# Graph network kernel: block joins in five parts, and SAGE's own linear part moved into the adjacency products

## The chip, the cores and the metric

The kernel runs on one core of a Trainium2 chip. The metric is the device time of one execution in microseconds (us), the median of several runs.

## The reference

The program is a stack of six graph layers over N = 3125 nodes with 128 features and E = 50000 edges, which are sorted by destination:

```
x  = x + relu(batchnorm(A x W0 + b))                 # GCN
x  = x + ffn(norm(attn(x, edge_attr)))               # 8 heads x 16, softmax over a node's edges
x  = x + gat1/gat2(x)                                # 3 heads x 128, then 1 head x 128
for l in (sage1, sage2):
    agg = segment_sum(h[src], dst) / max(cnt, 1)
    y   = agg @ Wl.T + h @ Wr.T + b
    h   = (y - mean) * (gamma / sqrt(var + eps)) + beta   # relu between the two
x  = x + h
```

attn, gat1 and gat2 have this form for each edge: a logit from the source's and the destination's rows, then, for every destination, sum(exp(logit - max) * row) / sum(exp(logit - max)).

## The kernel before, in words

The nodes are 25 tiles of 128; node stages go over them in seven turns (`TURNS`: one tile, then six times four). The edges are 392 blocks of 128 (`CH`), four blocks are a group (`GC`, 98 groups), two groups a pair (`NPR` = 49 ticks).

**An edge pass** (attn, gat1, gat2) is a software pipeline written out by hand. Each engine has a list of steps with an offset, for example `(terms, 2, 0)`, and `ticks` runs the whole list once for each pair: a step with 2 handles one group of the pair, one with 1 the pair. The steps of one pair in program order on DVE are `maxima` (the running maximum of a destination's logits, two scans, L2257 and L2263), `terms` of the even group (attn: L2224 adds the edge terms from PSUM to the gathered k and v rows, L2227 multiplies by the query rows from PSUM, L2243 reduces; gat: L2234 adds and L2247 applies the leaky slope), `difs` (L2270), `terms` of the odd group, and `messages` of the two groups of the pair before (L2286). PE makes the edge terms (`edge_terms`, L1573, attn only), spreads destination rows over edges (`dst_rows`, L1584 in attn, L1589 in gat), transposes the maxima (`max_t`, L1604) and sums the messages of a block (`sums`, L1613). ACT moves those sums out of PSUM (a copy, L1052), takes exponents (L1189), and stores them to memory (L1167). SP loads the constants of each group (L804, L811, L816, L819).

POOL gathers the source rows of a group from memory, four indirect loads (L1021). There are eight buffers of rows; the gather of group n waits for the messages of group n-8.

A destination's edges may run over several blocks. Each block leaves the sum and the maximum of its first and its last destination, and after the last group one **join** over all 392 blocks puts them together: PE collects the edge maxima (L1626), DVE makes the running maximum over the blocks and its differences (L2300 to L2316, `span` steps), ACT takes the exponent (L1221), SP loads the first and last rows of each block that were stored (L631), PE spreads the weights over partitions (L1642) and transposes the rows (L1659), and DVE runs for the denominators and for each chunk of 128 columns (attn and gat2 one chunk, gat1 three) two products, a scan, a product and a sum (L2328 to L2335). PE turns the result back (L1668, L1671), ACT copies it and SP stores it. Only then does POOL gather the result row of each node (L1030), and the node stage begins.

```
ticks([(maxima, 1, -1), (terms, 2, 0), (difs, 1, -1), (terms, 2, 1), (messages, 2, -2), (messages, 2, -1)])
```

**PSUM** has eight banks. In attn, bank 1 and bank 6 hold the edge terms of even and odd groups; in gat, banks 3 and 1 hold the destination rows of even and odd groups. A step that writes a bank waits for DVE's step of the group two before.

**SAGE** multiplies by the adjacency matrix in ten column chunks (`stream`, L1540; nine of them 100 matmuls long, in pieces of 5 tiles). After the product, a node stage goes over the turns: PE transposes h (L1690), multiplies the aggregate by Wl and the transposed h by Wr (L1809), ACT divides by the count (`mean_in`, L1355), DVE adds the two, multiplies by the batch norm's factor and adds its offset (L2537, L2381 twice). In sage1 the result is then split into three bfloat16 parts for the next product; in sage2 it is added to x and stored.

## Time and profile before

| | us |
|---|---|
| median of 3 runs | 3554.34 (3553.38 to 3568.37) |
| profiled execution, its own time | 3551.71 |
| its span | 3550.1 |

| stage | from | to |
|---|---|---|
| attn pass, its join | 660 | 1412, 1443.9 |
| gat1 pass, its join | 1571 | 2268.8, 2312.1 |
| gat2 pass, its join | 2445 | 3097, 3128.6 |
| gat2's node stage and the first SAGE product | 3128.6 | 3320 |
| sage1's node stage | 3338.0 | 3357.4 |
| second SAGE product | 3357.4 | 3507.7 |
| sage2's node stage, end | 3525.5 | 3550.1 |

Busy: PE 69%, DVE 40%, POOL 38%, ACT 27% of the span; the mean granted clock is 0.743 of full speed. The stage times are read off the timeline. A row of the timeline gives the start, the duration, engine, line and shape, and in brackets how long the engine stood idle before it and what released it ("remote" is a releaser that the trace doesn't identify).

### The profile page before, as it was taken

The numbers are of one execution on the slowest core, as the hardware profiler recorded it, in microseconds if no ns is written. First come the engines' busy times: TensorE is split into PE (matmuls) and PEld (weight loads), VectorE is DVE, ScalarE is ACT, GpSimd is POOL, SyncE is SP. The second block draws the span as 40 slices with busy tenths as digits, with TensorE's granted clock in tenths as the row PEclk, the third lists the DMA queues.
The fourth block names the chain that finished last, engine by engine and source line by source line (L and its number), as shares of the span: only waits on it lengthen the run. The fifth ranks groups of instructions, "written<-read, shape, count | busy, mean of one in ns | idle before, by whom it ended". The sixth has DMA issues, their size and how long they took to land.

```text
span 3550.1 us, 36582 instructions
## 1 busy us (share of the span) xinstructions
PE 2464.1 (69%) x12427; PEld 1828.4 (52%) x12427; DVE 1418.4 (40%) x3070; ACT 962.5 (27%) x2050; POOL 1354.0 (38%) x1417
## 2 busy tenths in 40 slices
PE   4999997377666766545677666664565655649998
PEld 3666665256555555333444444443564555526666
DVE  6756555244444455533333333431221212251423
ACT  3422223122222222442333333231221222220202
POOL 3000002645444553375555555045565555320000
PEclk9777788677777787667888888776555555569999
DMA  9388641456666674124555655322344444346362
GB/s 210 115 300 297 234 147 39 139 167 189 175 177 180 177 199 142 26 55 125 169 184 172 189 181 186 107 70 52 88 112 95 106 105 103 94 137 205 116 205 66
DMA packets 518595, 517.78 MB, mean 146 GB/s; under 512 B 154128, under 2 KB 463763, under 8 KB 517227
## 3 DMA queue, kind: packets, MB, share of 16 engines
q1 hardware_dynamic: 310349, 267.24, 24.9%
q0 software_dynamic: 50528, 115.22, 13.3%
q10 hardware_dynamic: 157534, 132.98, 11.9%
q8 instruction: 102, 1.67, 0.2%
q14 instruction: 82, 0.67, 0.1%
HBM read 301.13 MB, written 227.33 MB: 149 GB/s over the span
## 4 chain that ended last, share of the span: by engine, by line
PE 40%; another core or an unknown queue 25%; DVE 12%; issue 12%; ACT 6%; DMA 2%; POOL 1%; ACTq 0%; DVEq 0%; SPq 0%
PE ps L1613 9%; PE ps L1540 8%; PE ps L1434 6%; PE ps L1444 5%; ACT arena L1052 4%; DVE arena L2224 2%; DMA ends_gat<-arena 1%; PE ps L1522 1%; DVE arena L2286 1%; PE ps L1589 1%; PE ps L1573 1%; PE ps L1584 1%; DVE arena L1934 1%; DVE arena L2227 1%
## 5 line engine op out<-in xcount | busy, mean ns | idle before, releaser
L1052 ACT ACTIVATE arena<-ps 128x544 f32<-128x544 f32 (+9 forms) x591 | 485.9, 825 | 1746.1 <-remote 874.5
L1613 PE MATMUL ps<-arena 128*128 128x136 f32 (+2 forms) x2352 | 695.9, 460 | 376.3 <-ACT arena L1052 194.6
L1021 POOL DMA_INDIRECT arena<-t_gat,src_i x784 | 741.9, 946 | 537.1 <-DVE arena L2286 307.8
L1613 PEld LDWEIGHTS ps<-arena 128*128 128x128 f32 x2352 | 479.6, 269 | 516.4 <-issue 425.2
L1021 POOL DMA_INDIRECT arena<-t_attn,src_i x392 | 375.4, 958 | 344.1 <-DVE arena L2286 225.3
L2257 DVE TENSOR_TENSOR_SCAN arena<-arena,ps 64x128 f32<-64x128 f32 (+2 forms) x147 | 60.0, 408 | 803.0 <-remote 714.2
L1540 PE MATMUL ps<-arena 128*128 128x384 bf16 x1850 | 308.2, 331 | 37.6 <-issue 25.1
L1589 PEld LDWEIGHTS ps<-arena 128*128 128x128 f32 x1568 | 288.3, 268 | 45.2 <-issue 22.5
L1589 PE MATMUL ps<-arena 128*128 128x3 f32 (+1 forms) x1568 | 266.6, 292 | 15.7 <-issue 15.7
L1540 PEld LDWEIGHTS ps<-arena 128*128 128x128 bf16 x1850 | 183.1, 99 | 162.4 <-issue 46.0
L2286 DVE TENSOR_TENSOR arena<-arena,ps 128x1536 f32<-128x1536 f32 (+1 forms) x196 | 230.6, 1218 | 38.7 <-ACT arena L1189 30.1
L1444 PE MATMUL ps<-arena 128*128 128x100 bf16 x1176 | 224.4, 364 | 9.4 <-DVE arena L2064 9.2
L1434 PE MATMUL ps<-arena 128*128 128x385 bf16 x925 | 221.0, 413 | 0.0
L984 POOL TENSOR_TENSOR arena<-arena,r_L_gnn_gamma 128x512 f32<-128x512 f32 (+1 forms) x7 | 8.1, 1158 | 533.4 <-ACT arena L1252 533.3
L1444 PEld LDWEIGHTS ps<-arena 128*128 128x128 bf16 x1176 | 169.3, 145 | 58.9 <-DVE arena L2064 12.6
L1573 PE MATMUL ps<-w_e,arena 64*128 64x128 f32 x784 | 148.6, 324 | 59.7 <-issue 59.2
L1604 PE MATMUL ps<-ident,arena 64*128 64x64 f32 (+2 forms) x147 | 40.8, 278 | 201.1 <-DVE arena L2263 164.9
L2270 DVE TENSOR_TENSOR dif<-logit,ps 128x64 f32<-128x64 f32 (+2 forms) x147 | 27.4, 187 | 374.9 <-remote 199.5
L1052 ACT ACTIVATE arena<-same_b 128x512 f32<-128x512 bf16 x294 | 167.7, 619 | 29.6 <-DMA same_b<-same_hbm 28.7
L1573 PEld LDWEIGHTS ps<-w_e,arena 64*128 64x128 f32 x784 | 120.4, 222 | 88.5 <-issue 88.4
L1434 PEld LDWEIGHTS ps<-arena 128*128 128x128 bf16 x925 | 112.2, 121 | 102.9 <-issue 68.9
L1052 ACT ACTIVATE arena<-arena 128x512 bf16<-128x512 f32 (+4 forms) x208 | 64.3, 309 | 346.1 <-DVE arena L2524 247.8
(320 smaller groups left out, 2942.1 us busy)
## 6 DMA issues: line engine op xcount, KB each, us to landing
ends_gat<-arena ACTq DMA_DIRECT2D x98, 774.0 KB
arena<-adj_hbm SPq DMA_DIRECT2D x90, 640.0 KB, 4.2
same_b<-same_hbm SPq DMA_DIRECT2D x294, 128.0 KB
adj_hbm<-arena SPq DMA_DIRECT2D x9, 3200.0 KB, 11.8
ends_attn<-arena ACTq DMA_DIRECT2D x98, 272.0 KB
ends_gat<-arena ACTq DMA_DIRECT2D x98, 258.0 KB
arena<-edst SPq DMA_DIRECT2D x98, 256.0 KB, 4.2
starts_q<-zrow SPq DMA_DIRECT2D x28, 896.0 KB, 6.8
```

The lines of the kernel that those rows point to most:

```text
L1021: g.indirect_dma_start(out=row_b[:, n % RB, k, 0:row_tab[p].shape[1]], out_offset=None, in_=row_tab[p], in_offset=bass.IndirectOffsetOnAxi ...
L1052: return a.activation(o, i, ACT.Copy)
L1434: i = mm(bank(4 + n % 4)[:, 0:3 * D + 1], lhs, xs0[:, t, 0:3 * D + 1], start=t == 0, stop=t == NT - 1)
L1444: i = mm(ps[:, at:at + KEYS], hot_e[:, b % 3, :, e], hot_k[:, b % 3, :, e], start=True, stop=True)
L1540: m = mm(bank(ch % 2 * 4 + dl)[:, 0:3 * D], ring[:, u % RING, at:at + P], xs1[:, t, :, :].rearrange("p s c -> p (s c)"), start=t == 0, sto ...
L1573: i = mm(bank((1, 6)[g % 2])[:, k * D:(k + 1) * D], at_t[:, g % 2, k * P:(k + 1) * P], w_e[:, :], start=True, stop=True)
L1589: i = mm(ps[:, at:at + n_er], same_f[:, g % RB, k, :], er_c[:, g * GC + k, 0:n_er], start=True, stop=True)
L1604: nc.tensor.transpose(bank(2)[:, 256:256 + kh], mx[0:kh, i % 2, :], ident[0:kh, 0:kh])\
L1613: i = mm(o, same_f[:, g % RB, k, :], msg[:, g % 4, k * W:(k + 1) * W], start=True, stop=True)
L2224: tt(kv, kv, bc(bank((1, 6)[g % 2]).rearrange("p (k s c) -> p k s c", k=GC, s=1), [P, GC, 2, D]), ALU.add).then_inc(kve_done.sem, 1)
L2257: v.tensor_tensor_scan(fwd[0:kh, s, :], b[:, 0:P], bank(2)[0:kh, 0:P][:, ::-1], -BIG, ALU.add, ALU.max)\
L2286: tt(m[:, :, 0:heads * nc_].rearrange("p k (h c) -> p k h c", h=heads), rows_v, e, ALU.mult).then_inc(msg_done.sem, 1)
```

## The change

1. **Joins in five parts.** The blocks are cut at 72, 144, 216, 288 and 392. Four parts are joined inside the pass, at groups that `slots_of` lists; a step `mini` in each engine's list of the tick runs what is due there. A part is `edges` and the first transposes (PE), `tops` (DVE), the exponent (ACT), `mask` and the first `join` (DVE), then for each chunk transposes and spread (PE), a copy (ACT) and a `join` (DVE), then `back` (PE) and the rows' copy (ACT) and store (SP). A `carry` column hands the running values on. The fifth part, 104 blocks, is joined after the pass. SP loads the part's first and last rows in the pass and stores the results there.
2. **PSUM.** The parts inside the pass need a bank. In attn the edge terms now have only bank 1 and wait for L2224 of the group before; in gat1 the destination rows have only bank 3 and wait for L2234 of the group before. gat2 keeps both. In PE's list `max_t` moves ahead of these steps.
3. **SAGE.** The transposes of h and the product with Wr move ahead of the pieces of the first chunk (`own_lin`, called from `stream`). A new DVE step `keep` puts that product plus the batch norm's offset into h_sb, and the second chunk waits for the last `keep`. The batch norm's factor is multiplied into both weights once. What is left of the node stage is the product with Wl and one DVE instruction for each tile, which multiplies by the count's inverse and adds (`joined_in`); ACT's `mean_in` is gone, and in sage2 the product with Wl has two banks.

```diff
+PARTS = [(0, 72), (72, 144), (144, 216), (216, 288), (288, CH)]
+QP = len(PARTS)
+PW = max(b - a for a, b in PARTS)
...
+        def slots_of(p):
+
+            slots = {}
+
+            def put(g, *step):
+                slots.setdefault(g, []).append(step)
+
+            for q in range(QP - 1):
+                s = PARTS[q][1] // GC + 7
+                put(s, "edges", q, 0)
+                put(s + 1, "tops", q, 0)
+                put(s + 2, "exp", q, 0)
+                put(s + 3, "mask", q, 0)
+                put(s + 3, "join", q, 0)
+                for ch in range(1, col_chunks(p) + 1):
+                    put(s + 1 + 3 * ch, "cols", q, ch)
+                    put(s + 2 + 3 * ch, "copy", q, ch)
+                    put(s + 3 + 3 * ch, "join", q, ch)
+                s += 4 + 3 * col_chunks(p)
+                put(s, "back", q, 0)
+                put(s + 1, "rows", q, 0)
+            assert max(slots) < NG
+            return slots
...
+                def rows_for(q):
+                    b0, b1 = PARTS[q]
+                    g1 = b1 // GC
+                    for g in (g1 - 2, g1 - 1):
+                        sp.wait_ge(ends_out.of(g), ends_out.at(p, g))
+                    if part_at(p, q) > 1:
+                        sp.wait_ge(col_ps, col_at(p, q, 0) - 1)
+                    sp.dma_start(z_rows[0:b1 - b0, 0:W], v_ends[b0:b1, 0, :]).then_inc(s_rows, 16)
+                    sp.dma_start(f_rows[0:b1 - b0, 0:W], v_ends[b0:b1, P - 1, :]).then_inc(s_rows, 16)
+
+                def sums_out(q):
+                    b0, b1 = PARTS[q]
+                    sp.wait_ge(col_out, back_at(p, q, col_chunks(p)))
+                    sp.dma_start(ends[p][EP + P + b0:EP + P + b1, :], r_rows[0:b1 - b0, 0:W]).then_inc(s_rout, 16)
+
+                rows_at = {PARTS[q][1] // GC + 10: q for q in range(QP - 1)}
+                out_at = {PARTS[q][1] // GC + 19 + 3 * col_chunks(p): q for q in range(QP - 1)}
                 for g in range(NG):
                     if g % 2 == 0:
                         load_breaks(g // 2)
                     load_group(g)
-                for g in (NG - 2, NG - 1):
-                    sp.wait_ge(ends_out.of(g), ends_out.at(p, g))
-                sp.wait_ge(s_steps, c.at("z_in"))
...
                 def edge_terms(g):
                     pe.wait_ge(attr_sb_done.sem, attr_sb_done.at(p, g))
-                    if g >= 2:
-                        pe.wait_ge(kve_done.sem, kve_done.at(p, g, 2))
+                    if g >= 1:
+                        pe.wait_ge(kve_done.sem, kve_done.at(p, g, 1))
                     for k in range(GC):
-                        i = mm(bank((1, 6)[g % 2])[:, k * D:(k + 1) * D], at_t[:, g % 2, k * P:(k + 1) * P], w_e[:, :],
+                        i = mm(bank(1)[:, k * D:(k + 1) * D], at_t[:, g % 2, k * P:(k + 1) * P], w_e[:, :],
                                start=True, stop=True)
                     i.then_inc(e_done.sem, 1)
 
                 def dst_rows(g):
                     pe.wait_ge(same_f_done.sem, same_f_done.at(p, g))
-                    if g >= 2:
-                        pe.wait_ge(prod_done.sem, prod_done.at(p, g, 2))
+                    back = 1 if p == "gat1" else 2
+                    if g >= back:
...
-                    ticks([(logit_t, 1, -1), (sums, 2, -4), (attr_t, 2, 2), (edge_terms, 2, 1), (dst_rows, 2, 1),
-                           (max_t, 1, -1), (sums, 2, -3), (attr_t, 2, 3), (edge_terms, 2, 2), (dst_rows, 2, 2)])
+                    ticks([(logit_t, 1, -1), (sums, 2, -4), (attr_t, 2, 2), (max_t, 1, -1), (edge_terms, 2, 1),
+                           (dst_rows, 2, 1), (sums, 2, -3), (attr_t, 2, 3), (mini, 2, 0), (edge_terms, 2, 2),
+                           (dst_rows, 2, 2), (mini, 2, 1)])
...
+                    ticks([(logit_t, 1, -1), (sums, 2, -4), (max_t, 1, -1), (dst_rows, 2, 1), (sums, 2, -3),
+                           (mini, 2, 0), (dst_rows, 2, 2), (mini, 2, 1)])
...
-                ticks([(maxima, 1, -1), (terms, 2, 0), (difs, 1, -1), (terms, 2, 1), (messages, 2, -2), (messages, 2, -1)])
...
+                def tops(q, ch=0):
+                    b0, b1 = PARTS[q]
+                    n, k0, o = b1 - b0, span_at(p, q), Psum(p, q)
+
+                    def after(m):
+                        dve.wait_ge(span_dve, k0 + m)
+
+                    cpen, lpen = (span_m[0:heads, 2 + s, :] for s in range(2))
+                    R, M = run_x[0:heads, :], top_m[0:heads, 0:n]
+                    ex = lambda e: ex_h[0:heads, e, 1:n + 1]
+                    dve.wait_ge(edge_m_ps, part_at(p, q))
+                    after(0)
+                    if q == 0:
+                        v.memset(R[:, 0:1], -BIG)
+                        v.memset(ex_h[0:heads, :, 0:1], 0.0)
+                        v.memset(carry[:, :], 0.0).then_inc(span_dve, 1)
+                        after(1)
+                        v.tensor_tensor_scan(R[:, 1:n + 1], cpen[:, 0:n], o.last[:, 1:n + 1], -BIG, ALU.add, ALU.max)\
+                            .then_inc(span_dve, 1)
+                    else:
+                        m = PARTS[q - 1][1] - PARTS[q - 1][0]
+                        v.tensor_copy(o.last[:, 0:1], R[:, m:m + 1]).then_inc(span_dve, 1)
+                        after(1)
+                        v.tensor_tensor_scan(R[:, 0:n + 1], cpen[:, b0 - 1:b1], o.last, -BIG, ALU.add, ALU.max)\
+                            .then_inc(span_dve, 1)
+                    after(2)
+                    tt(ex(0), R[:, 0:n], R[:, 1:n + 1], ALU.subtract)
+                    tt(ex(1), o.last[:, 1:n + 1], R[:, 1:n + 1], ALU.subtract)
+                    tt(M, R[:, 0:n], lpen[:, b0:b1], ALU.add).then_inc(span_dve, 1)
+                    after(3)
+                    tt(M, M, o.first, ALU.max).then_inc(span_dve, 1)
+                    after(4)
...
+                def mask(q, ch=0):
+                    b0, b1 = PARTS[q]
+                    e = ex_h[0:heads, ::3, 1:b1 - b0 + 1]
+                    dve.wait_ge(span_exp, part_at(p, q))
+                    tt(e, e, span_m[0:heads, 0:2, b0:b1], ALU.mult).then_inc(span_dve, 1)
...
+                    dve.wait_ge(col_ps, col_at(p, q, ch))
+                    dve.wait_ge(span_dve, k0)
+                    if col_at(p, q, ch) > 1:
+                        dve.wait_ge(col_done, col_at(p, q, ch) - 1)
+                    if ch == 0 and part_at(p, q) > 1:
+                        dve.wait_ge(col_back, back_at(p, q, 0) - 1)
+                    if ch >= 2 and q == QP - 1:
+                        dve.wait_ge(col_back, back_at(p, q, ch - 2))
+                    held = carry[0:parts_n, ch:ch + 1]
+                    v.tensor_copy(u[:, 0:1], held)
+                    tt(u[:, 1:n + 1], e[:, 1, 1:n + 1], z, ALU.mult)
+                    tt(t, e[:, 2, 1:n + 1], f, ALU.mult).then_inc(span_dve, 1)
+                    dve.wait_ge(span_dve, k0 + 1)
+                    v.tensor_tensor_scan(sc[:, 0:n + 1], e[:, 0, 0:n + 1], u[:, 0:n + 1], 0.0, ALU.mult, ALU.add)\
+                        .then_inc(span_dve, 1)
+                    dve.wait_ge(span_dve, k0 + 2)
+                    tt(u[:, 1:n + 1], e[:, 3, 1:n + 1], sc[:, 0:n], ALU.mult)
+                    v.tensor_copy(held, sc[:, n:n + 1]).then_inc(span_dve, 1)
+                    dve.wait_ge(span_dve, k0 + 3)
+                    tt(t, t, u[:, 1:n + 1], ALU.add).then_inc(col_done, 1)
+
+                def mini(g):
+                    in_slots(p, g, tops=tops, mask=mask, join=join)
+
+                ticks([(maxima, 1, -1), (terms, 2, 0), (difs, 1, -1), (terms, 2, 1), (mini, 2, 0), (messages, 2, -2),
+                       (messages, 2, -1), (mini, 2, 1)])
+                tops(QP - 1)
...
+                own, at_piece = own_lin(i), [0, 2, 6, 8, 10, 12, 14]
                 for n, (ch, t0, t1) in enumerate(PIECE):
+                    if n <= NT // HI:
+                        for step, j in own[at_piece[n]:at_piece[n + 1]]:
+                            step(j)
+                    if (ch, t0) == (1, 0):
+                        pe.wait_ge(dve_o.sem, dve_o.at(("gat2", "sage1")[i], "keep"))
...
+                def la(j):
+                    if p == "sage1" and j >= 1:
+                        pe.wait_ge(dve_o.sem, dve_o.at(p, "yh", j - 1))
+                    if p == "sage2" and j >= 2:
+                        pe.wait_ge(dve_o.sem, dve_o.at(p, "yx", j - 2))
+                    b = 7 if p == "sage1" else 6 + j % 2
+                    for k, t in enumerate(range(*TURNS[j])):
+                        m = mm(part(bank(b), k), part(agg_t, t), sage_t[:, 2 * i, :], start=True, stop=True)
+                    m.then_inc(pe_o.sem, 1)
+
...
+            for i in range(2):
+                k = tt(sage_t[:, 2 * i:2 * i + 2, :], sage_t[:, 2 * i:2 * i + 2, :],
+                       bc(bn_a[:, i:i + 1, :], [P, 2, D]), ALU.mult)
+            k.then_inc(s_sage, 1)
+
+            def own_sum(i, stage, after):
+                def step(j):
+                    dve.wait_ge(pe_o.sem, pe_o.at(stage, "lh", j))
+                    dve.wait_ge(dve_o.sem, dve_o.at(after, "r2", j))
+                    tt(tiles(h_sb, j), in_bank(6)(j), fb(bn_b[:, i, :], j), ALU.add).then_inc(dve_o.sem, 1)
+                return step
 
...
+                def joined_in(b, t_out):
+                    def step(j):
+                        dve.wait_ge(pe_o.sem, pe_o.at(p, "la", j))
+                        if p == "sage2":
+                            dve.wait_ge(s_sage, 2)
+                        for k, t in enumerate(range(*TURNS[j])):
+                            n = stt(t_out[:, t, :], part(bank(b(j)), k), cnt_r[:, t:t + 1], t_out[:, t, :], ALU.mult, ALU.add)
+                        n.then_inc(dve_o.sem, 1)
+                    return step
+
```

PE, one tick of attn before and after (in the rows L1613 is `sums`, L1565 `attr_t`, L1573 `edge_terms`, L1584 `dst_rows`, L1604 `max_t`, L1597 `logit_t`; after, these are L1751, L1702, L1710, L1722, L1742, L1735). Before:

```order
L1597 MATMUL ps<-ident,logit 64x128
L1613 MATMUL ps<-arena 128x136 x4
L1565 MATMUL ps<-ident,arena 64x128 x4
L1573 MATMUL ps<-w_e,arena 128x128 x4
L1584 MATMUL ps<-arena 128x128 x4
L1604 MATMUL ps<-ident,arena 128x64
L1613 MATMUL ps<-arena 128x136 x4
L1565 MATMUL ps<-ident,arena 64x128 x4
L1573 MATMUL ps<-w_e,arena 128x128 x4
L1584 MATMUL ps<-arena 128x128 x4
```

After, in a tick with the end of a part (L1809 and L1810 are `back`):

```order
L1735 MATMUL ps<-ident,logit 64x128
L1751 MATMUL ps<-arena 128x136 x4
L1702 MATMUL ps<-ident,arena 64x128 x4
L1742 MATMUL ps<-ident,arena 128x64
L1710 MATMUL ps<-w_e,arena 128x128 x4
L1722 MATMUL ps<-arena 128x128 x4
L1751 MATMUL ps<-arena 128x136 x4
L1702 MATMUL ps<-ident,arena 64x128 x4
L1809 MATMUL ps<-ident,ht 72x128
L1810 MATMUL ps<-ident,ht 72x8
L1710 MATMUL ps<-w_e,arena 128x128 x4
L1722 MATMUL ps<-arena 128x128 x4
```

The first `edge_terms` and `dst_rows` of a tick stood ahead of `max_t` and now stand behind it; `back` stands between the second `sums` and the second `edge_terms`.

DVE, the end of one tick of attn, where L2286 is `messages`. Before:

```order
L2270 TENSOR_TENSOR dif<-logit,ps 128x64
L2224 TENSOR_TENSOR arena<-arena,ps 128x1024
L2227 TENSOR_TENSOR arena<-arena,ps 128x512
L2243 TENSOR_REDUCE logit<-arena 128x32
L2286 TENSOR_TENSOR arena<-arena 128x4x128 x2
L2257 SCALAR_TENSOR_TENSOR arena<-arena,ps 64x128
```

After, in the tick with part 0's `tops` (L2460 to L2483); `messages` is L2445 there:

```order
L2460 MEMSET arena 8x1
L2461 MEMSET arena 8x4
L2462 MEMSET arena 128x4
L2464 SCALAR_TENSOR_TENSOR arena<-span_m,ps 8x72
L2473 TENSOR_TENSOR arena<-arena 8x72
L2474 TENSOR_TENSOR arena<-ps,arena 8x72
L2475 TENSOR_TENSOR arena<-arena,span_m 8x72
L2477 TENSOR_TENSOR arena<-arena,ps 8x72
L2479 TENSOR_TENSOR arena<-ps,arena 8x72
L2480 TENSOR_TENSOR arena<-arena 8x72
L2483 TENSOR_SCALAR arena<-arena 8x4x72
L2445 TENSOR_TENSOR arena<-arena 128x4x128 x2
```

The eleven rows of `tops` come ahead of the messages of the tick.

PE around the node stage of sage1 before (L1690 transposes h, L1809 multiplies), and the product behind it:

```order
L1809 MATMUL ps<-sage_t,arena 128x128 x4
L1809 MATMUL ps<-sage_t,ht 128x128 x4
L1690 MATMUL ps<-ident,h_sb 128x128 x4
L1809 MATMUL ps<-sage_t,arena 128x128 x4
L1809 MATMUL ps<-sage_t,ht 128x128 x4
L1540 MATMUL ps<-arena 128x384 x925
```

PE at the first chunk of the first product after (L1644 transposes h, L1654 multiplies by Wr, L1677 is the product):

```order
L1644 MATMUL ps<-ident,h_sb 128x128 x5
L1677 MATMUL ps<-arena 128x384 x20
L1654 MATMUL ps<-sage_t,ht 128x128
L1644 MATMUL ps<-ident,h_sb 128x128 x4
L1654 MATMUL ps<-sage_t,ht 128x128 x4
L1644 MATMUL ps<-ident,h_sb 128x128 x4
L1677 MATMUL ps<-arena 128x384 x20
L1654 MATMUL ps<-sage_t,ht 128x128 x4
```

The product of 20 matmuls (five tiles) of the first chunk now stands between a turn's own product and the next.

## Rows read from the trace of the kernel before

**Rows 1.** The page: the clock by slices, and POOL's gather groups of part 5
```profile
PEclk9777788677777787667888888776555555569999
...
L1021 POOL DMA_INDIRECT arena<-t_gat,src_i x784 | 741.9, 946 | 537.1 <-DVE arena L2286 307.8
...
L1021 POOL DMA_INDIRECT arena<-t_attn,src_i x392 | 375.4, 958 | 344.1 <-DVE arena L2286 225.3
```

**Rows 2.** Busy time by stretch: the three joins (stretch, length, engines, clock, DMA)
```profile
core 0: us, PE busy (x) PEld busy (x) DVE busy (x) ACT busy (x) POOL busy (x), PEclk, DMA share, GB/s
1414.00:1444.00 30.00, 13.57 (x69) 9.02 (x68) 12.39 (x22) 5.69 (x6) 0.10 (x1) 0.50 0.14 40
2268.80:2312.10 43.30, 27.13 (x105) 16.39 (x104) 18.68 (x32) 9.16 (x9) 0.07 (x1) 0.57 0.24 79
3099.00:3128.60 29.60, 13.17 (x67) 8.60 (x66) 16.07 (x36) 5.65 (x6) 0.09 (x1) 0.50 0.14 39
```

**Rows 3.** Timeline in attn (start, us, engine, line, tiles, [idle before <-releaser])
```profile
1013.71 2.07 PE L1584 MATMUL ps<-arena 128*128 128x128 f32 x8 [0.34 <-issue]
...
1040.45 0.95 POOL L1021 DMA_INDIRECT arena<-t_attn,src_i  x1 [0.30 <-issue]
...
1042.82 0.37 PE L1573 MATMUL ps<-w_e,arena 64*128 64x128 f32 x1 [1.03 <-issue]
...
1044.25 1.62 PE L1584 MATMUL ps<-arena 128*128 128x128 f32 x6 [0.15 <-issue]
...
1044.36 0.41 DVE L2257 TENSOR_TENSOR_SCAN arena<-arena,ps 64x128 f32<-64x128 f32 x1 [14.45 <-remote]
...
1045.15 1.19 DVE L2224 TENSOR_TENSOR arena<-arena,ps 128x1024 f32<-128x1024 f32 x1
...
1045.80 0.37 PE L1604 MATMUL ps<-ident,arena 64*128 64x64 f32 x1
...
1046.10 2.18 PE L1613 MATMUL ps<-arena 128*128 128x136 f32 x8
...
1047.98 1.22 DVE L2224 TENSOR_TENSOR arena<-arena,ps 128x1024 f32<-128x1024 f32 x1
...
1049.06 1.16 PE L1573 MATMUL ps<-w_e,arena 64*128 64x128 f32 x8
...
1049.23 0.69 DVE L2227 TENSOR_TENSOR arena<-arena,ps 128x512 f32<-128x512 f32 x1
...
1051.99 0.94 POOL L1021 DMA_INDIRECT arena<-t_attn,src_i  x1 [10.59 <-DVE arena L2286]
```

**Rows 4.** Timeline in gat1, one critical tick
```profile
1834.09 0.99 PE L1589 MATMUL ps<-arena 128*128 128x3 f32 x8
...
1837.31 0.24 PE L1604 MATMUL ps<-ident,arena 24*128 24x24 f32 x1 [2.23 <-DVE arena L2263]
...
1837.70 0.17 DVE L2234 TENSOR_TENSOR z_b<-arena,ps 128x12 f32<-128x12 f32 x1
...
1840.90 0.95 POOL L1021 DMA_INDIRECT arena<-t_gat,src_i  x1 [7.20 <-DVE arena L2286]
```

**Rows 5.** Timeline in gat2, POOL's first gather after a wait
```profile
2700.90 0.95 POOL L1021 DMA_INDIRECT arena<-t_gat,src_i  x1 [6.40 <-DVE arena L2286]
```

**Rows 6.** Timeline of attn's join
```profile
1414.94 2.78 PE L1626 MATMUL ps<-arena,ident 64*8 64x49 f32 x32
...
1419.23 0.14 DVE L2303 TENSOR_TENSOR arena<-arena 8x1 f32<-8x1 f32 x1
...
1425.74 5.56 PE L1642 MATMUL ps<-arena,spread 8*128 8x392 f32 x8 [8.02 <-issue]
...
1431.23 2.77 PE L1659 MATMUL ps<-ident,arena 98*8 98x98 f32 x16
...
1438.11 0.57 DVE L2333 TENSOR_TENSOR arena<-arena 128x391 f32<-128x391 f32 x1
...
1443.90 0.95 POOL L1030 DMA_INDIRECT arena<-ends_attn,end_i  x1 [63.74 <-SPq L836]
```

**Rows 7.** Timeline of gat1's join, its first and last step and SP's load
```profile
2268.93 1.60 PE L1626 MATMUL ps<-arena,ident 24*3 24x49 f32 x32
...
2275.11 0.83 SPq L631 DMA_DIRECT2D arena<-ends_gat  x2
...
2312.03 0.95 POOL L1030 DMA_INDIRECT arena<-ends_gat,end_i  x1 [88.93 <-SPq L836]
```

**Rows 8.** Timeline of the SAGE node stages
```profile
3353.68 0.60 PE L1690 MATMUL ps<-ident,h_sb 128*128 128x128 f32 x4
...
3356.24 1.13 ACT L1355 ACTIVATE h_sb<-ps,cnt_r 128x128 f32<-128x128 f32 x4
...
3356.40 1.16 PE L1809 MATMUL ps<-sage_t,ht 128*128 128x128 f32 x8 [1.23 <-ACT ht L1052]
...
3357.39 2.93 PE L1540 MATMUL ps<-arena 128*128 128x384 bf16 x17
...
3545.29 0.69 DVE L2381 TENSOR_TENSOR x_sb<-h_sb,x_sb 128x512 f32<-128x512 f32 x1
```

462 lines of the change are left out of this document (258 added, 204 removed).

## Prediction

> **What bounds the kernel now.** I began with the page: no engine is busy over 69% of the span, so waits set the time in most stages. The costliest group of waits is POOL's ahead of its gathers, which DVE's messages end: 307.8 us in the two gat passes and 225.3 us in attn [rows 1]. The timeline of one tick of attn shows what such a wait is. POOL issues 16 gathers of four groups back to back, 0.95 us each and 0.30 us apart, 20 us in all; the last one starts at 1040.45. Meanwhile DVE stands still for 14.45 us, until 1044.36, 3 us after POOL's last gather has been issued; ACT and SP start again within 0.1 us of it. Then comes a tick that nothing covers, which I call the critical tick. DVE goes through its maxima (1044.36), the terms of the even group (1045.15) and of the odd group (1047.98 and 1049.23) with no gap over 0.1 us. POOL goes on after the first message, having waited 10.59 us [rows 3]. The next tick runs under the new burst. So a period of two ticks is a burst plus that wait, 30.6 us: what is added ahead of the messages of a critical tick lengthens the pass, and what is added elsewhere fits into DVE's 14 us. In gat1 the wait is 7.20 us [rows 4], in gat2 6.40 us [rows 5]. By the sums of rows 1, attn has about 225.3 / 10.59 = 21 such periods; gat1, which also has shorter waits, I put at 20, gat2 at 20.
>
> The joins are the second bound: 30.0, 43.3 and 29.6 us in which POOL, whose gathers the next stage needs, is idle [rows 2]. They are a chain of small steps through PE, DVE, ACT and SP, with PE at half clock (0.50 to 0.57).
>
> **The joins, after.** What is left after the pass handles 104 of 392 blocks. In attn the join runs from 1414.94 to POOL's gather at 1443.90. A DVE step takes 0.57 us for 391 elements and 0.14 us for one, so 1.1 ns for each element more; 104 elements take 0.25 us. The spread of the weights (5.56 us) shrinks to 1.6 us, the transposes of the rows (2.77 us for 16) to 0.7 us for 4 [rows 6]. The first step (2.78 us for 32 records) has as many matmuls as before, and the store and its landing (2.8 us, from ACT's copy to the gather) stay. My sum for what is left is 2.8 + 3.4 for the maxima + 1.6 + 0.7 + 0.6 for ACT's copy + 3.2 for DVE's two runs + 0.4 for turning back + 2.8 = 15.5 us, so 13.5 us saved. gat2 has the same form: 13.5 us. gat1 goes from 2268.93 to 2312.03; its rows are loaded from 2275.11 on [rows 7], and with four runs on DVE I come to 23 us, 20 saved. Together **-47 us**. If all but the first step and the store scaled with the blocks, it were -61; if only DVE and the spread did, -35.
>
> **The parts inside the passes.** By the same line a step of 72 elements takes 0.22 us, so `tops` is about 2.1 us on DVE, `mask` 0.25, and a `join` 1.45. Their slots fall now in a critical tick, ahead of the messages, now in a covered one. Counting slots against the ticks of the trace, three `tops` and two `mask` with `join` are exposed in attn (7 us less what falls behind messages), 11 us in gat1, which has three chunks, and 8 us in gat2: **+26 us**. The ends are 0 (every such tick turns into a covered one) and 75, the whole DVE work of 12 parts. I take 26, since rows 3 show DVE with no gap in a critical tick, and a long gap behind it. PE's and ACT's parts of this, and SP's two loads and one store for each part, I cost at nothing: PE, ACT and SP all stand still in the bursts as DVE does. If their cover is gone, see the last rival. Behind PE's wait for SP's load stand `edge_terms` and `dst_rows` of the next tick, and DVE's terms wait for those.
>
> **One bank and the new order on PE.** This I take to be the largest cost. Before, PE did the edge terms and destination rows of the odd group inside the stall: the edge terms end at 1043.19 and the destination rows at 1045.87, when DVE has just started [rows 3]. Now the edge terms of the odd group wait for DVE's L2224 of the even group, which ends at 1046.34, and stand behind `max_t`. PE has then been idle for the whole stall and is at half clock: eight records take 2.07 us there, against 1.16 us at full clock [rows 3]. So edge terms end at 1048.5 and destination rows at 1050.6 (half clock) or 1049.7 (full). DVE's L2224 of the odd group moves from 1047.98 to 1048.6, its L2227 from 1049.23 to between 1049.9 and 1050.7. The messages come 0.7 to 1.5 us later; I take 1.4, because in the rows PE stays at half clock through the sums that follow (2.18 us at 1046.10). That is 21 x 1.4 = 29 us, and 4 us in the ticks at the end of the pass, where POOL has no more gathers: +33. In gat1 the destination rows of the odd group took 0.99 us at 1834.09, in the stall. Now they follow `max_t`, which ends at 1837.55, and end at 1838.7; DVE's L2234 of that group started at 1837.70 [rows 4]. That is 1.1 us a period, 20 periods: +22. gat2 keeps two banks: 0. Together **+55 us**, between 0 and 75.
>
> **SAGE.** The work on PE is moved, not removed: 0.60 us of transposes and 1.16 us of products with Wr for four tiles, 11 us for a whole pass [rows 8]. What it lands in, the first chunk of the first product, is slack only where PE waits for the tiles to be ready, about 3 us. It then delays the second chunk by about 7 us in each product, since the second chunk also waits for the last `keep`. In sage1 those 11 us and ACT's 1.13 us a turn leave the node stage, where the first product's piece starts at 3357.39; I have the second chunk 1 us later than now at best and 7 later at worst, and take 7. sage2's node stage (3525.5 to the last sum at 3545.29) loses the transposes, ACT's step and three of four DVE steps of 0.69 us; 8.6 us stay, -12. Sum 7 + 7 - 12 = **+3 us** (from -10 to +10).
>
> **Sum**: -47 + 26 + 55 + 3 = +37. The profiled execution took 3551.7 us, 2.6 below the median of the runs; on the median this gives 3554.3 + 37 = 3591 us. About 0.5%, 18 us, is what a measurement of this kernel can tell from no change.
>
> **Rivals.**
> *All of it is covered (faster, 3510).* The work in the passes and PE's later steps cost nothing and only the joins get shorter: -47 + 3 = -44. It decides if the odd group's operands are in PSUM when DVE comes to them, that is if PE's two steps together take under 2.6 us (1046.34 to 1048.98), and if the parts' slots fall in covered ticks. For it: DVE is only 40% busy. Against it: the half clock in every stall [rows 3], and the slots. Chance 0.25.
> *PE runs at full clock after the stall (same, 3558).* Edge terms then end at 1047.6 and destination rows at 1048.8, both before DVE wants them, and attn's 33 us go; gat1's 22 stay: +4. Chance 0.2.
> *Descriptors are held up (3601).* In the trace a gather issued in a burst takes 958 ns in attn, where DVE works more, and 946 ns in gat [rows 1], so DVE's work holds POOL up by little. If the copies and scalar steps of the parts stopped POOL for their length, that would be about 0.9 us for a part in attn and gat2 and 1.4 in gat1, 13 us less the exposed third, +10 on the sum. The Trainium skill ("SBUF — State Buffer", section "Who interferes with whom") states such a lock: a DVE instruction in a two-port mode, as copies and tensor_scalar can be, shuts GpSimd out for its whole length. Rows 1 agree only in that tensor_tensor work costs next to nothing; what a copy does, none of them shows. Chance 0.05.
> *The loaded rows come late (slower, 3680).* PE waits in a tick for rows that SP loads while the gathers fill the queues, and these are released only when a burst is over, as DVE is in rows 3. With 12 parts and up to a critical tick (7.4 us) for each, +90. It decides if SP's load of a part is issued less than a burst ahead of PE's step. Chance 0.1.
>
> **Chances.** The forecast gets 0.4. Faster: the first rival's 0.25 and 0.05 from a forecast in which gat1 and the parts cost less: 0.3. Same: the second rival's 0.2, and 0.05 of the forecast. Slower: 0.45. The range of 3508 to 3630 goes from the first rival to the forecast with PE's term at its upper end (+75); it leaves out most of the last rival and of the still larger savings.
>
> **What would show it.** Right: joins of about 15, 23 and 15 us; POOL's wait in attn 12.0 us instead of 10.6 and in gat1 8.3; gaps of 0.6 us ahead of L2224's and L2227's successors in the critical tick with PE as releaser; edge terms of the odd group behind `max_t` at 2.07 us; sage2's node stage 12 us shorter; the first chunk of each product longer. Wrong: POOL's waits unchanged, or PE's steps at 1.16 us there (then the second rival), or waits on SP's loads in the passes.

## The result, and the profile after

The changed kernel takes **3622.12 us** (median of 4 runs, 3620.23 to 3626.14) against 3556.52 us before on the same chip: the ratio is 1.0188 (95% interval 1.0156 to 1.0219), 66 us slower. The profiled execution has a span of 3619.0 us, 68.9 more than before.

I cut both traces at the same events of the timeline: POOL's first gather of a pass, DVE's last message of it, POOL's first gather of the results, and PE's first matmul of the second chunk and last one of each product.

| stretch, us | before | after | difference |
|---|---|---|---|
| attn pass, first gather to last message | 747.5 | 805.1 | +57.6 |
| gat1 pass | 689.2 | 733.9 | +44.7 |
| gat2 pass | 647.5 | 661.9 | +14.4 |
| last message to first gather of the results, attn | 35.4 | 19.1 | -16.3 |
| the same, gat1 | 51.1 | 30.3 | -20.8 |
| the same, gat2 | 35.8 | 19.8 | -16.0 |
| gat2's results to the second chunk | 57.6 | 68.9 | +11.3 |
| end of the first product to the second chunk of the second | 53.6 | 63.0 | +9.4 |
| end of the second product to the end | 42.5 | 30.4 | -12.1 |
| everything else | 1189.9 | 1186.6 | -3.3 |

The passes lose 116.7 us, the joins win 53.1, SAGE loses 8.6.

The page after shows the clock of the slices and the gather groups, which answer to [rows 1]:

```profile
PEclk9777788677777777676878877877555555569999
...
L1111 POOL DMA_INDIRECT arena<-t_gat,src_i x784 | 741.6, 946 | 592.4 <-DVE arena L2445 363.5
...
L1111 POOL DMA_INDIRECT arena<-t_attn,src_i x392 | 373.2, 952 | 404.2 <-DVE arena L2445 285.3
```

POOL waits 285.3 us for messages in attn, 60 more than before, and 363.5 in the gat passes, 56 more. The gathers themselves take as long as before (946 and 952 ns).

The joins by stretch (the columns are those of [rows 2]), from the last message on:

```profile
1468.30:1487.20 18.90, 9.00 (x64) 7.16 (x62) 5.41 (x24) 4.68 (x8) 0.00 (x0) 0.50 0.24 68
2347.90:2378.20 30.30, 15.46 (x84) 10.73 (x84) 8.40 (x39) 6.50 (x11) 0.01 (x1) 0.70 0.35 121
3169.10:3188.90 19.80, 9.12 (x65) 7.27 (x64) 8.11 (x35) 4.61 (x8) 0.00 (x0) 0.50 0.22 62
```

Inside attn's join, from the timeline (start, us, engine, line):

```profile
1474.42 0.96 PE L1763 MATMUL ps<-arena,ident 64*8 64x13 f32 x32
...
1475.42 0.15 DVE L2468 COPY ps<-arena 8x1 f32<-8x1 f32 x1 [7.31 <-PE ps L1763]
...
1476.00 0.26 DVE L2473 TENSOR_TENSOR arena<-arena 8x104 f32<-8x104 f32 x1
...
1478.78 2.03 PE L1779 MATMUL ps<-arena,spread 8*128 8x105 f32 x8 [3.40 <-DVE arena L2489]
...
1480.75 0.85 PE L1798 MATMUL ps<-ident,arena 104*8 104x104 f32 x4
...
1487.25 0.94 POOL L1120 DMA_INDIRECT arena<-ends_attn,end_i  x1 [47.08 <-DMA ends_attn<-arena]
```

From PE's first step to POOL's gather it is 12.8 us, where it was 28.96 [rows 6]. A DVE step of 104 elements takes 0.26 us, the spread 2.03 and the transposes 0.85 us. PE's first step writes 13 columns instead of 49, so its 32 records take 0.96 us, not 2.78.

A tick of attn that nothing covers, again from the timeline, which answers to [rows 3]:

```profile
1227.53 0.94 POOL L1111 DMA_INDIRECT arena<-t_attn,src_i  x1 [0.30 <-issue]
...
1230.80 0.41 DVE L2416 TENSOR_TENSOR_SCAN arena<-arena,ps 64x128 f32<-64x128 f32 x1 [13.16 <-remote]
...
1231.59 1.19 DVE L2383 TENSOR_TENSOR arena<-arena,ps 128x1024 f32<-128x1024 f32 x1
...
1231.72 0.36 PE L1742 MATMUL ps<-ident,arena 64*128 64x64 f32 x1 [7.75 <-DVE arena L2422]
...
1232.92 2.04 PE L1710 MATMUL ps<-w_e,arena 64*128 64x128 f32 x8 [0.84 <-DVE arena L2383]
...
1234.89 2.07 PE L1722 MATMUL ps<-arena 128*128 128x128 f32 x8
...
1237.06 1.22 DVE L2383 TENSOR_TENSOR arena<-arena,ps 128x1024 f32<-128x1024 f32 x1 [2.71 <-PE ps L1722]
...
1241.08 0.95 POOL L1111 DMA_INDIRECT arena<-t_attn,src_i  x1 [12.60 <-DVE arena L2445]
```

POOL's last gather of the burst starts at 1227.53, DVE goes on at 1230.80. PE does the edge terms of the odd group (L1710) when DVE's L2383 of the even group has let go of the bank, at half clock, and the destination rows (L1722) behind them, at half clock too. DVE's second L2383 has been idle for 2.71 us when it starts at 1237.06, released by L1722. POOL waits 12.60 us here, where it was 10.59. PE's times are close to those of the forecast; what the forecast left out is that DVE waits for L1722 ahead of its second L2383, so this starts 4.3 us after the first one's end instead of 2.3.

The end of the first chunk of the second product, and the end of the program:

```profile
3450.88 1.05 PE L1654 MATMUL ps<-sage_t,ht 128*128 128x128 f32 x8
...
3452.81 1.13 PE L1654 MATMUL ps<-sage_t,ht 128*128 128x128 f32 x8 [0.87 <-DVE h_sb L2692]
3453.98 0.69 DVE L2692 TENSOR_TENSOR h_sb<-ps,bn_b 128x512 f32<-128x512 f32 x1 [1.31 <-PE ps L1654]
...
3454.73 1.47 PE L1677 MATMUL ps<-arena 128*128 128x384 bf16 x8 [0.79 <-DVE h_sb L2692]
```

```profile
3606.60 2.27 PE L1973 MATMUL ps<-sage_t,arena 128*128 128x128 f32 x18 [0.93 <-DVE arena L2267]
...
3612.77 2.16 DVE L2751 SCALAR_TENSOR_TENSOR x_sb<-ps,cnt_r,x_sb 128x128 f32<-128x128 f32 x8 [0.22 <-PE ps L1973]
```

PE does a turn's product with Wr (L1654), waits 0.87 us for the last `keep` but one, and 0.79 us for the last (L2692), before the second chunk begins at 3454.73. In the node stage of sage2 one DVE instruction (L2751) of 0.27 us for each tile is left.

### The profile page after: what moved, and what is told of

Read it like the earlier page. It is cut to its first block, busy times and chain, and to the rows that moved or that the text cites. A ratio compares the mean times of both kernels' runs of the same rounds, so it can differ in the third digit from the quotient of the medians.

```text
span 3619.0 us, 38289 instructions
## 1 busy us (share of the span) xinstructions
PE 2503.3 (69%) x12995; PEld 1879.1 (52%) x12995; DVE 1451.4 (40%) x3454; ACT 950.5 (26%) x2056; POOL 1350.9 (37%) x1417
## 4 chain that ended last, share of the span: by engine, by line
PE 40%; another core or an unknown queue 27%; DVE 15%; issue 10%; ACT 4%; DMA 2%; POOL 1%; DVEq 0%; ACTq 0%; SPq 0%
PE ps L1751 8%; PE ps L1677 8%; PE ps L1537 6%; PE ps L1547 5%; DVE arena L2445 3%; DVE arena L2383 3%; PE ps L1727 3%; ACT arena L1142 2%; PE ps L1722 2%; PE ps L1710 1%; PE ps L1625 1%; DVE arena L2093 1%; DVE arena L2416 1%; DVE arena L2386 1%
## 5 line engine op out<-in xcount | busy, mean ns | idle before, releaser
L1142 ACT ACTIVATE arena<-ps 128x544 f32<-128x544 f32 (+7 forms) x610 | 479.3, 794 | 1882.9 <-remote 880.9
L1111 POOL DMA_INDIRECT arena<-t_gat,src_i x784 | 741.6, 946 | 592.4 <-DVE arena L2445 363.5
L1751 PE MATMUL ps<-arena 128*128 128x136 f32 (+2 forms) x2352 | 697.0, 458 | 209.9 <-ACT arena L1142 102.8
L1751 PEld LDWEIGHTS ps<-arena 128*128 128x128 f32 x2352 | 485.1, 271 | 346.6 <-issue 271.0
L1111 POOL DMA_INDIRECT arena<-t_attn,src_i x392 | 373.2, 952 | 404.2 <-DVE arena L2445 285.3
L1727 PEld LDWEIGHTS ps<-arena 128*128 128x128 f32 x1568 | 294.2, 277 | 61.8 <-issue 51.7
L1727 PE MATMUL ps<-arena 128*128 128x3 f32 (+1 forms) x1568 | 284.9, 304 | 45.2 <-issue 27.5
L1677 PE MATMUL ps<-arena 128*128 128x384 bf16 x1850 | 306.9, 329 | 8.8 <-DVE rec L2622 7.2
L1710 PE MATMUL ps<-w_e,arena 64*128 64x128 f32 x784 | 149.4, 347 | 178.0 <-DVE arena L2383 151.6
L1742 PE MATMUL ps<-ident,arena 64*128 64x64 f32 (+2 forms) x147 | 40.8, 277 | 316.8 <-DVE arena L2422 280.7
L1677 PEld LDWEIGHTS ps<-arena 128*128 128x128 bf16 x1850 | 182.3, 99 | 130.7 <-issue 12.2
L2445 DVE TENSOR_TENSOR arena<-arena,ps 128x1536 f32<-128x1536 f32 (+1 forms) x196 | 230.1, 1214 | 18.0 <-ACT arena L1279 13.5
L1710 PEld LDWEIGHTS ps<-w_e,arena 64*128 64x128 f32 x784 | 130.1, 248 | 193.4 <-ACT arena L1142 101.0
L2383 DVE TENSOR_TENSOR arena<-arena,ps 128x1024 f32<-128x1024 f32 x98 | 118.0, 1204 | 258.6 <-remote 215.3
L1742 PEld LDWEIGHTS ps<-ident,arena 64*128 64x128 f32 (+2 forms) x147 | 23.3, 159 | 365.8 <-DVE arena L2422 302.4
```

Of the source, the lines that this page charges most:

```text
L1111: g.indirect_dma_start(out=row_b[:, n % RB, k, 0:row_tab[p].shape[1]], out_offset=None, in_=row_tab[p], in_offset=bass.IndirectOffsetOnAxi ...
L1142: return a.activation(o, i, ACT.Copy)
L1677: m = mm(bank(ch % 2 * 4 + dl)[:, 0:3 * D], ring[:, u % RING, at:at + P], xs1[:, t, :, :].rearrange("p s c -> p (s c)"), start=t == 0, sto ...
L1710: i = mm(bank(1)[:, k * D:(k + 1) * D], at_t[:, g % 2, k * P:(k + 1) * P], w_e[:, :], start=True, stop=True)
L1727: i = mm(ps[:, at:at + n_er], same_f[:, g % RB, k, :], er_c[:, g * GC + k, 0:n_er], start=True, stop=True)
L1751: i = mm(o, same_f[:, g % RB, k, :], msg[:, g % 4, k * W:(k + 1) * W], start=True, stop=True)
```

## The experiments

The jobs ran on several chips, on which the kernel before has different times: 3529 us in the first job (e1, e2, e3, e5), 3523 in the second (a0, e4, e6, e7), 3555 in the third (e8, e9, e11, e12). Every ratio is against runs of the kernel before on the same chip; traces are compared inside one job where that is possible. The table gives the length of the three passes in each trace, from the first gather to the last message, as above. Each kernel has one trace, and single runs of one kernel lie up to 48 us apart, so differences of a few us between two traces say little.

| kernel | median us | ratio (95% interval) | attn | gat1 | gat2 |
|---|---|---|---|---|---|
| e1 bank only | 3528.74 | 1.0008 (0.9980 to 1.0036) | 749.7 | 694.2 | 630.2 |
| e2 SAGE only | 3533.99 | 1.0019 (0.9986 to 1.0052) | 743.2 | 687.3 | 629.0 |
| e3 wait behind the addition | 3563.05 | 1.0108 (1.0079 to 1.0138) | 776.4 | 727.2 | 647.7 |
| e5 parts behind the messages | 3533.37 | 1.0040 (0.9985 to 1.0095) | 767.1 | 714.7 | 643.9 |
| a0 the changed kernel again | 3572.25 | 1.0127 (1.0093 to 1.0160) | 778.0 | 730.5 | 649.5 |
| e4 e3, destination rows first | 3544.41 | 1.0062 (1.0035 to 1.0089) | 756.0 | 731.2 | 644.2 |
| e6 e4 and e5 | 3529.25 | 1.0017 (0.9996 to 1.0038) | 761.3 | 716.3 | 646.7 |
| e7 e6 without SAGE | 3521.38 | 1.0000 (0.9975 to 1.0025) | 764.3 | 721.0 | 643.8 |
| e8 e1 and DVE's instructions | 3600.46 | 1.0120 (1.0089 to 1.0151) | 776.1 | 699.7 | 645.9 |
| e9 e1 and PE's instructions | 3650.43 | 1.0261 (1.0230 to 1.0292) | 786.6 | 723.4 | 654.7 |
| e11 e1 and SP's loads | 3586.24 | 1.0098 (1.0065 to 1.0131) | 774.4 | 692.9 | 645.8 |
| e12 all three | 3635.64 | 1.0221 (1.0188 to 1.0254) | 792.3 | 726.8 | 655.3 |

**e1: only the shared bank.** The kernel before with the change's hunks on the two banks and PE's new order, and nothing else:

```diff
-                    if g >= 2:
-                        pe.wait_ge(kve_done.sem, kve_done.at(p, g, 2))
+                    if g >= 1:
+                        pe.wait_ge(kve_done.sem, kve_done.at(p, g, 1))
...
-                    ticks([(logit_t, 1, -1), (sums, 2, -4), (attr_t, 2, 2), (edge_terms, 2, 1), (dst_rows, 2, 1),
-                           (max_t, 1, -1), (sums, 2, -3), (attr_t, 2, 3), (edge_terms, 2, 2), (dst_rows, 2, 2)])
+                    ticks([(logit_t, 1, -1), (sums, 2, -4), (attr_t, 2, 2), (max_t, 1, -1), (edge_terms, 2, 1),
+                           (dst_rows, 2, 1), (sums, 2, -3), (attr_t, 2, 3), (edge_terms, 2, 2), (dst_rows, 2, 2)])
```

> The kernel before with only the shared bank and the new order on TensorE in attn and gat1; joins and SAGE as before. Theory 1 (the odd group's operands come late in the tick that nothing covers, 10.1 us in the trace of the changed kernel against 7.5 before): attn's gathers from first to last take about 45 to 50 us longer than the 719 us of before, gat1's about 30 longer than 651, gat2's 627 stay, in all about +75 to +85 us. Rival (the parts joined inside the passes are what lengthens them): the gathers of attn and gat1 together grow by less than 40 us.

The ratio is 1.0008. Theory 1, which is the prediction's, falls on this chip. e2 has the passes of before, on the same chip: against it attn is 6.5 us longer, gat1 6.9, gat2 1.2. The gather groups of the two pages, of e1 first:

```profile
L1021 POOL DMA_INDIRECT arena<-t_gat,src_i x784 | 740.4, 944 | 526.1 <-DVE arena L2290 297.1
...
L1021 POOL DMA_INDIRECT arena<-t_attn,src_i x392 | 371.1, 947 | 345.2 <-DVE arena L2290 225.8
```

```profile
L1023 POOL DMA_INDIRECT arena<-t_gat,src_i x784 | 740.5, 944 | 522.1 <-DVE arena L2312 292.2
...
L1023 POOL DMA_INDIRECT arena<-t_attn,src_i x392 | 372.8, 951 | 339.9 <-DVE arena L2312 217.3
```

POOL's waits in attn come to 225.8 us in the one and 217.3 in the other. In e1's timeline the uncovered tick does take 10.1 us from its maxima to its last message, as in the changed kernel, and 7.5 in the kernel before. But POOL now waits 35 times for an average of 6.5 us, where it waited 26 times for 8.4 in e2. The pass goes over to bursts of two groups for long stretches: in attn e1 has 31 bursts of two groups and 7 of four, e2 13 and 16. Ticks that begin with DVE idle for over 6 us, which is how I count uncovered ticks, are 10 in e1 and 17 in e2. So the tick became as long as its rows say, and the number of such ticks fell. That the pattern is what hides the cost is not shown by this: the first trace of the changed kernel has the same 31 and 7 in attn, and waits 285.3 us.

**e2: only SAGE.** The hunks of `own_lin`, `keep`, `joined_in` and the folded factor on the kernel before:

```diff
+                    if n <= NT // HI:
+                        for step, j in own[at_piece[n]:at_piece[n + 1]]:
+                            step(j)
+                    if (ch, t0) == (1, 0):
+                        pe.wait_ge(dve_o.sem, dve_o.at(("gat2", "sage1")[i], "keep"))
```

> The kernel before with only the SAGE part of the change. By the trace of the changed kernel its second chunks start 11.4 and 9.3 us later and sage2's end comes 12.2 us sooner: +8.5 us if nothing else in that kernel takes part, so about 3563 to 3566 against 3556. Rival (the joins' part moves the first product's start, and SAGE alone costs nothing or gains): within 3 us of before or faster.

1.0019, with an interval that holds both. The trace decides: against e1, on the same chip and without SAGE's part, gat2's results to the second chunk take 59.8 us instead of 51.6, the first product's end to the second chunk of the second 62.1 instead of 53.6, and the end 30.4 instead of 42.5. That is +8.2 +8.5 -12.1 = +4.6 us. The last two of these repeat within about 2 us in every trace. The first one varies with or without SAGE's part: from 51.6 to 62.4 us in the seven traces without it and from 59.8 to 69.3 in the seven with it. The means differ by 8.2 us, so +8.2 is a fair size for it, and the +11.3 of the first comparison is partly chance. Later, e6 and e7 differ by this part alone: 3529.25 and 3521.38.

**e3: DVE's wait behind the addition.**

```diff
-                    dve.wait_ge(dst_done.sem, dst_done.at(p, g))
+                    if p != "attn":
+                        dve.wait_ge(dst_done.sem, dst_done.at(p, g))
...
                         dve.wait_ge(kve_done.sem, kve_done.at(p, g))
+                        dve.wait_ge(dst_done.sem, dst_done.at(p, g))
                         tt(prod[:, :, :], row_b[:, r, :, 0:D], bank((3, 7)[g % 2]).rearrange("p (k c) -> p k c", k=GC),
```

> The changed kernel with VectorE's wait for the destination rows put behind the addition of the edge terms in attn. Theory 1 with its detail (the addition at 1237.06 stood waiting for the destination rows that ended at 1236.96, though its edge terms were there at 1234.96): the uncovered tick shortens by about 1.2 us of its 10.1, attn's gathers by 20 to 28 us of 777. Rival (the tick is bound by the bank alone): under 5 us.

I had compared with the 777.2 us of gathers in attn on the first chip; here they take 744.3. But a0, the changed kernel on another chip, has 745.1. The two ratios, 1.0108 and 1.0127, have overlapping intervals, and attn is 1.6 us shorter in e3's trace than in a0's. The uncovered tick did get shorter, as expected: 8.9 us in e3 and 10.1 in a0 (medians). The pass didn't follow. So no gain from the wait's place can be seen, and most of the 33 us comes with the chip.

**e5: the parts' steps on DVE behind the messages.**

```diff
-                ticks([(maxima, 1, -1), (terms, 2, 0), (difs, 1, -1), (terms, 2, 1), (mini, 2, 0), (messages, 2, -2),
-                       (messages, 2, -1), (mini, 2, 1)])
+                ticks([(maxima, 1, -1), (terms, 2, 0), (difs, 1, -1), (terms, 2, 1), (messages, 2, -2),
+                       (messages, 2, -1), (mini, 2, 0), (mini, 2, 1)])
```

> The changed kernel with VectorE's steps of the parts always behind the messages of a tick. Theory 1 (the parts' work ahead of the messages costs what falls in uncovered ticks, put at 7 us in attn, 11 in gat1, 8 in gat2): 15 to 26 us faster. Rival 2 (the parts cost by breaking the pairing of bursts and by waits on rows that SP loads, not by VectorE's work): under 8 us faster.

**a0: the changed kernel once more.**

> The changed kernel once more, for a comparison on the chip of this job. On the chip of its own first runs it was 1.0188 times the kernel before. Theory 2 (the shared bank alone costs nothing, the parts' steps ahead of the messages cost the most): ratio again 1.015 to 1.022, and attn's gathers 30 us or more longer than in the run with the parts' steps behind the messages (733 us). Rival (the first job's chip made the difference between the two): attn's gathers near 735 and a ratio near 1.004.

a0 has 1.0127 and e5 1.0040: moving DVE's steps takes about 31 us off (0.87% of 3530). By the traces it is 10.9 us in attn, 15.8 in gat1 and 5.6 in gat2, 32 in all. The two were on different chips, and e5's interval is wide (one of its four runs took 3570 us, the others 3522 to 3536) and touches a0's. On one chip, e4 and e6 below differ by the same move: 15 us. POOL's waits in the gat passes, of a0 and of e5:

```profile
L1111 POOL DMA_INDIRECT arena<-t_gat,src_i x784 | 742.3, 947 | 577.9 <-DVE arena L2445 343.8
```

```profile
L1111 POOL DMA_INDIRECT arena<-t_gat,src_i x784 | 740.8, 945 | 558.3 <-DVE arena L2445 331.3
```

This is the prediction's term for the parts' exposed work, put at 26 us, which lies between the two.

**e4: the destination rows of the odd group first**, with e3's edit.

```diff
-                    ticks([(logit_t, 1, -1), (sums, 2, -4), (attr_t, 2, 2), (max_t, 1, -1), (edge_terms, 2, 1),
-                           (dst_rows, 2, 1), (sums, 2, -3), (attr_t, 2, 3), (mini, 2, 0), (edge_terms, 2, 2),
+                    ticks([(logit_t, 1, -1), (sums, 2, -4), (attr_t, 2, 2), (dst_rows, 2, 1), (max_t, 1, -1),
+                           (edge_terms, 2, 1), (sums, 2, -3), (attr_t, 2, 3), (mini, 2, 0), (edge_terms, 2, 2),
```

> The changed kernel with VectorE's wait for the destination rows behind the addition, as in e3, and in attn TensorE's destination rows of the odd group ahead of the transposed maxima, so that they are made while VectorE stands still. Theory 1: the uncovered tick of attn goes from 8.9 to about 8.2 us, 10 to 15 us less than e3 (3563). Theory 2 (what e1 showed: later operands alone do not lengthen the pass, since the bursts then fall into pairs of groups): under 8 us less than e3.

1.0062 against a0's 1.0127 on the same chip: 23 us. In the traces attn is 22.0 us shorter, and gat1, which the edit doesn't touch, the same within 0.7. So late destination rows do cost something in attn once the parts are in the pass, though e1, without the parts, hardly shows it. Why, is open. a0 has 23 bursts of two groups in attn, where e1 has 31 and e4 has 39, which would fit parts that break up the stretches in which e1 hid the longer tick. But the changed kernel's first trace has 31, as e1, so the pattern alone doesn't decide it, and no run tests it.

**e6: e4 and e5 together.**

> e4 and e5 together: the changed kernel with the destination rows first, the wait behind the addition, and the parts' steps behind the messages. If the two costs add: e5 was 60 us below the changed kernel's ratio and e3 28; together at most 75, so 20 us faster than before, ratio 0.993 to 0.997. If they overlap (both are the same uncovered tick): as e5, 1.00 to 1.004.

1.0017: 39 us below a0, where the two alone took 23 and 31. So the two gains overlap by some 15 us, as far as 31 can be trusted across two chips.

**e7: e6 without SAGE.**

> e6 without the SAGE part of the change. If SAGE costs what its second chunks show (+11.4 +9.3 -12.2 = +8.5 us), this is 8.5 us faster than e6, ratio about 0.992. Rival (SAGE costs nothing outside the noise): as e6 within 3 us.

1.0000. The medians differ by 7.9 us, as expected, though the intervals overlap. No kernel of this study is faster than the one before: what is left of the parts' cost in the passes is as large as what the joins win.

**e8, e9, e11, e12: the parts' instructions without their results.** e5 still has passes that are 66 us longer than e2's on the same chip (2125.7 against 2059.5 in sum). To see whose work that is, I put instructions of the parts' number, sizes and places into e1, one engine at a time. Nobody reads what they write, nobody waits for them, and the joins are made behind the pass as before:

```diff
+                def mini(g):
+                    o = bank(1 if p == "gat1" else 6)
+                    for name, b1, ch in part_slots(p).get(g, []):
+                        if name == "edges":
+                            for s in range(2):
+                                for k in range(PB):
+                                    mm(o[0:heads, s * 128 + k:s * 128 + 72:PB], ident[0:kh, k * heads:(k + 1) * heads],
+                                       edge_m[0:kh, 0:9, s], start=True, stop=True)
...
+                    if g in rows_at:
+                        b1 = rows_at[g]
+                        for h in (b1 // GC - 2, b1 // GC - 1):
+                            sp.wait_ge(ends_out.of(h), ends_out.at(p, h))
+                        sp.dma_start(pw_z[0:72, 0:W], v_ends[b1 - 72:b1, 0, :]).then_inc(part_in, 16)
```

> The kernel with only the shared bank (e1: attn 716, gat1 656, gat2 610 us from the first to the last gather) plus, at the parts' slots and behind the messages, VectorE instructions of the parts' number and sizes whose results nobody reads; joins as before. e5 with the real parts behind the messages took 733, 677 and 621. Theory 3 (VectorE's work is not covered even there, since its sum of 21, 33 and 21 us goes with the growth of 17, 21 and 11): +10 us or more in each of attn and gat1, in all +30 to +50 us, ratio 1.009 to 1.015. Rival 3 (the growth comes from TensorE's steps and from waits between the engines and on the loaded rows): within 8 us of e1, ratio below 1.003.

> e1 plus TensorE instructions of the parts' number and sizes into the bank that is free, at the parts' places in TensorE's list, waiting for nobody; joins as before. Theory 3: within 8 us of e1. Rival 3a (TensorE's steps ahead of the edge terms and destination rows delay VectorE): +15 us or more over the three passes.

> e1 plus SP's loads of each part's first and last rows with their waits for the stores of the part's last groups, into a buffer that nobody reads; joins as before. Theory 3: within 8 us of e1. Rival 3b (SP stands waiting for the stores and its later loads of the groups come late): +15 us or more over the three passes.

> e8, e9 and e11 together, on e1; joins as before. If the three costs explain the growth in the passes, the passes grow as in e5, by about 50 us over e1, and the ratio is about 1.014. If waits between the engines for the parts' results are the cost, less than half of it.

The job's chip was a slower one, and e1 was not on it; e11 is the nearest to it. This matters for the verdicts. e8, e11 and e1 have the shared bank, and e8 and e11 have 1.0120 and 1.0098 where e1 has 1.0008 on its own chip. Either DVE's instructions and SP's loads each cost about 1%, or the bank does on this chip. The traces speak for the bank: against the kernel before on the first chip (3557 us there, 3555 here), attn is 28.6 us longer in e8 and 26.9 in e11, gat1 10.5 and 3.7, and gat2, whose bank and order are those of before, 1.6 and 1.7 shorter. e1 wasn't run on this chip, so this stays open, and with it what SP's loads cost (rival 3b).

Against e11, DVE's instructions add 8.6 us to the sum of the passes (1.7 + 6.8 + 0.1), PE's add 51.6 us (12.2 + 30.5 + 8.9). e12 has 9.7 us more than e9 in the passes, and its ratio, 1.0221, is no larger than e9's 1.0261 within the intervals. e8's ratio lies in the range that theory 3 gave, but by the traces DVE's instructions have 8.6 us of it. So theory 3 falls as the main cause, and so does its rival as I had put it, that waits for the parts' results are the cost: **PE's steps alone, waiting for nothing, lengthen the passes by 52 us against e11 and by 43 against e8.** The medians are 64 and 50 us apart.

The gather groups, e11 first:

```profile
L1055 POOL DMA_INDIRECT arena<-t_gat,src_i x784 | 740.2, 944 | 546.4 <-DVE arena L2324 323.9
...
L1055 POOL DMA_INDIRECT arena<-t_attn,src_i x392 | 370.8, 946 | 371.1 <-DVE arena L2324 255.6
```

```profile
L1044 POOL DMA_INDIRECT arena<-t_gat,src_i x784 | 742.2, 947 | 575.9 <-DVE arena L2335 348.9
...
L1044 POOL DMA_INDIRECT arena<-t_attn,src_i x392 | 372.5, 950 | 386.7 <-DVE arena L2335 267.6
```

The timeline of gat2 shows how. In e11 a tick begins behind a burst, POOL goes on, and the next tick's maxima (L2295) follow PE's transposed logits (L1632):

```profile
2779.52 0.41 DVE L2295 TENSOR_TENSOR_SCAN arena<-arena,ps 8x128 f32<-8x128 f32 x1 [15.74 <-remote]
...
2782.81 0.94 POOL L1055 DMA_INDIRECT arena<-t_gat,src_i  x1 [6.38 <-DVE arena L2324]
...
2784.08 0.37 PE L1632 MATMUL ps<-ident,logit 128*8 128x128 f32 x1
...
2784.49 0.41 DVE L2295 TENSOR_TENSOR_SCAN arena<-arena,ps 8x128 f32<-8x128 f32 x1 [1.83 <-PE ps L1632]
```

The same place in e9, in the tick at whose end PE has the first step of a part (L1646 and L1649, in the free bank):

```profile
2822.13 0.41 DVE L2306 TENSOR_TENSOR_SCAN arena<-arena,ps 8x128 f32<-8x128 f32 x1 [15.09 <-remote]
...
2825.42 0.95 POOL L1044 DMA_INDIRECT arena<-t_gat,src_i  x1 [6.30 <-DVE arena L2335]
...
2826.75 0.94 PE L1646 MATMUL ps<-arena,ident 8*1 8x9 f32 x32
...
2827.63 0.40 PE L1649 MATMUL ps<-ident 72*1 72x72 f32 x2
...
2827.82 0.42 PE L1621 MATMUL ps<-ident,logit 128*8 128x128 f32 x1
...
2834.05 0.41 DVE L2306 TENSOR_TENSOR_SCAN arena<-arena,ps 8x128 f32<-8x128 f32 x1 [8.79 <-remote]
...
2836.95 0.60 ACT L1075 ACTIVATE arena<-ps 128x516 f32<-128x516 f32 x1 [9.96 <-remote]
...
2839.40 0.95 POOL L1044 DMA_INDIRECT arena<-t_gat,src_i  x1 [4.27 <-DVE arena L2335]
```

PE's step (0.94 and 0.40 us) puts the transposed logits (L1621) 5.69 us behind the tick's start instead of 4.56. DVE's maxima could follow them at about 2828.2. They start at 2834.05, after 8.79 us of idleness.

The view calls the releaser remote, because what raised the semaphore had ended long before. But the trace also holds the time at which each semaphore was raised: that of L1621 is raised at 2834.03, 5.8 us after the matmul's end. ACT's step at 2836.95 follows the semaphore of PE's L1637, raised at 2836.93, 7.0 us after that step's end. In e11 the semaphore of the transposed logits (L1632) is raised at 2784.47, 0.02 us after their end. So DVE and ACT stand still because PE's semaphores come late. In the kernel before it is the same: all 52 of DVE's idle times over 6 us ahead of the maxima end when the semaphore of the transposed logits (L1597) is raised, 5.3 to 15.5 us after the matmul's recorded end.

PE itself goes on in a burst, slowly. In the kernel before, at the end of the burst of [rows 3], a matmul comes every 1.4 us, and no wait that the trace knows lies between:

```profile
1040.02 0.37 PE L1573 MATMUL ps<-w_e,arena 64*128 64x128 f32 x1 [1.13 <-issue]
...
1041.42 0.37 PE L1573 MATMUL ps<-w_e,arena 64*128 64x128 f32 x1 [1.03 <-issue]
```

A delay of a little over 1 us has thus turned a semaphore that came at once into one that was held. The transposed logits end 1.6 us after the burst's first gather in e11 and 2.8 us after it in e9. Time alone doesn't decide it, since e11's L1639, which ends 5 us after the first gather, is answered at once by DVE. What holds a semaphore, and whether the delay or the 34 more PE instructions bring it on, no run shows.

The next tick begins 11.9 us behind this one instead of 5.0. It is so at the first steps of the second, third and fourth part of gat2; behind the first part's it is 22.5 us instead of 9.6. The pass wins most of it back, since the burst that follows starts sooner: POOL's next wait is 4.27 us. Of the 8.9 us of gat2, 1.4 are there before the first part and 7.4 come with the four parts, about 2 us for each. In gat1, where e9 is 30.5 us longer, the delays are less regular, and I haven't taken them apart.

## Why the prediction was right, and where it was wrong

- **Direction and size.** Forecast was +37 us, 3591, with a range up to 3630; measured are +66 and 3622. Slower, given 0.45, came out.
- **The joins, -47.** Measured -53.1: 16.3, 20.8 and 16.0. attn and gat2 are better by 2.8 and 2.5 us. Two terms are mis-sized. PE's first step I kept at 2.8 us because the number of matmuls is the same: it takes 0.96 us. The store and its landing I kept at 2.8 us: from SP's issue, which follows ACT's copy at once, to POOL's gather it is now 1.9. In attn the two make up the 2.7 us between the forecast's 15.5 and the measured 12.8.
- **DVE's exposed steps, +26.** Right in kind: 32 us by the traces of e5 and a0, on two chips, and 15 by the medians of e4 and e6 on one.
- **One bank and PE's order, +55: over-priced, above all in gat1.** The tick itself was under-priced in attn, since I overlooked that DVE waits for the destination rows ahead of the addition: it is 10.1 us instead of 7.5, where I had 8.9. But that tick was multiplied by 21 periods that I took to be alike. The trace before has 18 stalls over 6 us ahead of the maxima in attn, and 11 bursts of two groups beside 17 of four; e1 has 10 such stalls. e1's passes are 14.6 us longer than e2's, 1.2 of them in gat2, which e1 leaves as it was, and nothing shows in the medians. On the slower chip, which is as fast as the one of the forecast, e11 and e8 have attn 27 to 29 us longer, against 33 forecast, and gat1 4 to 11, against 22. So attn's term may be about right there and too large on e1's chip, and gat1's is too large on both. How much of e11 and e8 is the bank stays open, since e1 wasn't on that chip.
- **PE's steps of the parts, at nothing: the step that failed.** "PE, ACT and SP all stand still in the bursts as DVE does" was the reason. PE doesn't stand still there; it is slow, and its semaphores come late. And its steps don't fall into the stall: they stand at the end of the tick ahead of the transposed logits, on the way to the next tick's maxima. They are worth 43 to 52 us by e9's trace, the largest cost of the change.
- **The drain of 4 us in attn.** It can't be seen: from the last gather to the last message it is 28.0 us, 28.3 before. But in the other traces this stretch is 23 to 34 us, so 4 us would not stand out.
- **SAGE, +3.** Measured +8.6 in the first comparison, +4.6 in e2. The second chunks are 9.4 and 11.3 us late, and 8.2 and 8.5 in e2, where I took 7; sage2's -12.1 is as put. The two waits for `keep` at the end of the chunk (0.87 and 0.79 us) are of the size of e2's excess.
- **The rivals.** "All of it is covered" is refuted by the waits of POOL. "PE runs at full clock" is refuted by L1710 and L1722 at 2.04 and 2.07 us. "The loaded rows come late": PE's idle time ahead of its transposes of the loaded rows (L1798) is 3.1, 1.1 and 1.2 us in the three passes of the changed kernel, where +90 was the rival's price. e11 tests SP's side alone, since PE doesn't wait for its rows; its passes are 28.9 us longer than those of the first chip's kernel before, the bank included. "Descriptors are held up": gathers take 952 and 946 ns after, 958 and 946 before. The means could hide the 13 us, but the single gathers don't show it either: a copy or a tensor_scalar of a part lies beside a gather 45 times in the changed kernel's passes, and one of these gathers takes over 1 us. The Trainium skill ("SBUF — State Buffer", "Who interferes with whom") has the lock for copies in a two-port mode. These copies are of one element a partition, and whether any of them is in such a mode the trace doesn't say.

So the sum was near in part by luck: 81 us were forecast for the passes and 117 came. The bank was over-priced and PE's steps were left out. By adding up numbers of three chips, the 117 are some 30 for bank and SP, 52 for PE's steps and 32 for DVE's, which is 114; that they meet so closely is chance too, as 43 for PE and 15 for DVE are as good.

## What to carry to other kernels

In a pipeline whose period is a burst and a tick that it can't cover, ask of each added instruction what the next tick waits for on that engine, not how busy the engine is: 1.3 us of PE ahead of a transposed row moved the start of the next tick in gat2 from 5.0 to 11.9 us, of which about 2 us remained in the pass. A longer uncovered tick must not be multiplied by the old number of bursts, as the pattern of bursts itself changes. Work that is taken from the end of a pass into it should stand behind everything that the next tick begins with: e5 and e6 show it for DVE. For PE it follows from e9's timeline, but no run moved PE's steps.

## What the runs showed of the hardware that was not expected

- The same program takes 3523 to 3557 us on different chips, and the changed kernel's ratio was 1.0188 on the first and 1.0127 on the second job's (their intervals just overlap). In gat2 the gathers from first to last took 627.0 us in the kernel before on the first chip and 609.8 in e1, which has the same gat2, on another, at the same 0.95 us for a gather.
- While POOL issues a burst of gathers, PE's semaphores can be held: in the kernel before, at the burst of [rows 3], the semaphores of L1584, L1597, L1613 and L1565 are raised one after the other from 1044.30 to 1044.49. L1597 had run at 1028.76, L1565 at 1034.45. SP, DVE and ACT go on 0.02 us after the first three of them, about 3 us after the burst's last gather. A burst alone doesn't stop DVE: in e11 it goes through a whole tick, 2784.49 to 2789.83, beside POOL's gathers. Whether PE's matmuls ran late or only their semaphores came late, the trace can't tell, since their ends are modelled, and no run took it apart.
